# Block keys by DMA, exponential per head and dequantisation shared out between two chunks, in the stage ahead of an attention recurrence

## What is computed

```python
x = x + xattn(layernorm(x), ctx, ctx, mask)      # softmax(q k / 4 + mask) v
x = x + ffn(layernorm(x), gate, up, down)        # int4 weights: q * s, s per 128 inputs
x = x + recurrence(ctx, layernorm(x), lens)      # 256 steps, one after the other
x = x + experts(layernorm(x))                    # 16 experts, top 2
```

## Time and profile before

| what | value |
|---|---|
| median of 3 runs (lowest, highest) | 1523.16 us (1520.36, 1537.06) |
| profiled execution | 1518.94 us |
| its span, first to last instruction | 1516.8 us |
| mean granted clock of TensorE | 0.93 |
| busy over the span | PE 1395.5 us (92%), DVE 943.9 (62%), ACT 544.3 (36%), POOL 275.1 (18%) |
| part A | 0 to 144.43 us |
| part B | 144.43 to 262.83 us |
| part C up to the recurrence's first matmul | 262.83 to 301.66 us |

### The profile page before, as it was taken

One profiled execution on the slowest core, in us unless ns is written; L12 is line 12 of the kernel. 1 busy time (PEld: TensorE's weight loads), 2 busy tenths in 40 slices (PEclk: granted clock), 3 DMA queues, 4 the chain that ended last, 5 costly groups with the idle time before them and its releaser, 6 DMA issues.

```text
span 1516.8 us, 43579 instructions
## 1 busy us (share of the span) xinstructions
PE 1395.5 (92%) x17408; PEld 919.4 (61%) x17408; DVE 943.9 (62%) x4478; ACT 544.3 (36%) x2143; POOL 275.1 (18%) x743
## 2 busy tenths in 40 slices
PE   4743887899999999999999999999999999999988
PEld 2533666466665676666666765556666666666546
DVE  4898455366665666675666657766655566566643
ACT  1343132134333344333334434443433333333321
POOL 3334222211111111111011111231110011111111
PEclk8565797999999999999999999999998999999989
DMA  8623000000000000000000001210000000000000
GB/s 278 240 90 90 0 1 4 1 2 2 3 2 2 2 2 2 3 2 2 2 2 2 2 19 45 58 37 2 2 16 2 2 2 9 9 2 3 9 9 14
DMA packets 19551, 37.06 MB, mean 24 GB/s; under 512 B 8436, under 2 KB 11683, under 8 KB 19348
## 3 DMA queue, kind: packets, MB, share of 16 engines
q1 hardware_dynamic: 19348, 34.28, 6.9%
HBM read 32.18 MB, written 2.10 MB: 23 GB/s over the span
## 4 chain that ended last, share of the span: by engine, by line
PE 83%; DVE 9%; issue 3%; ACT 2%; SPq 1%; POOL 1%; DMA 0%; DVEq 0%; ACTq 0%; POOLq 0%
PE bank L1921 9%; PE bank L1842 9%; PE bank L1635 9%; PE bank L1864 8%; PE bank L1652 6%; PE bank L1896 6%; PE bank L1673 4%; PE bank L1870 4%; PE bank L1618 3%; PE bank L1878 3%; PE bank L1905 3%; PE bank L1884 2%; PE bank L1612 2%; PE bank L1566 2%; PE bank L1518 2%
## 5 line engine op out<-in xcount | busy, mean ns | idle before, releaser
L1842 PE MATMUL bank<-ctx_lgs,identb 128*128 128x512 f16 (+2 forms) x685 | 190.9, 356 | 0.0
L1921 PE MATMUL bank<-ker_mem,uh 128*128 128x128 f32 x1020 | 184.3, 304 | 0.7 <-DVE ker_mem L1121 0.4
L1921 PEld LDWEIGHTS bank<-ker_mem,uh 128*128 128x128 f32 x1020 | 137.0, 194 | 66.1 <-DVE ker_mem L1121 48.9
L1635 PE MATMUL bank<-xT,wbig 128*128 128x256 f16 x1008 | 162.9, 275 | 0.0
L693 POOL TENSOR_TENSOR sscale<-ex,rinv 128x8 f32<-128x8 f32 x256 | 51.0, 199 | 506.8 <-DVE rinv L1106 506.8
L1439 ACT ACTIVATE xs<-gat 64x8 f32<-64x8 f32 x255 | 52.9, 207 | 244.2 <-DVE gat L1117 244.2
L1425 ACT ACTIVATE ker_mem<-bank 128x128 f16<-128x128 f32 x256 | 71.0, 278 | 184.8 <-PE bank L1864 184.8
L1430 ACT ACTIVATE eh<-bank,nmx 128x8 f16<-128x8 f32 x256 | 68.5, 268 | 172.4 <-PE bank L1887 172.4
L689 POOL COPY sscale<-s 64x4 f32<-64x4 f32 x256 | 59.0, 230 | 388.6 <-DVE s L1136 388.6
L1652 PE MATMUL bank<-wbig,interT 128*128 128x512 f16 x378 | 125.6, 399 | 0.0
L1121 DVE TENSOR_TENSOR ker_mem<-inv,ahn 128x128 f32<-128x128 f32 x510 | 124.0, 285 | 0.1
(11 more groups left out here) (238 smaller groups left out, 3290.9 us busy)
## 6 DMA issues: line engine op xcount, KB each, us to landing
wbig<-d_gate_qT SPq DMA_DIRECT2D x4, 896.0 KB, 9.9
wbig<-d_up_qT SPq DMA_DIRECT2D x4, 896.0 KB, 20.7
wbig<-d_down_qT SPq DMA_DIRECT2D x1, 3584.0 KB, 31.5
x_sb<-d_x SPq DMA_DIRECT2D x16, 128.0 KB, 6.0
d_out<-x_sb SPq DMA_DIRECT2D x16, 128.0 KB, 2.3
sscale<-d_gate_sT SPq DMA_DIRECT2D x2, 896.0 KB, 8.3
sscale<-d_up_sT SPq DMA_DIRECT2D x2, 896.0 KB, 4.3
work<-d_g1T SPq DMA_DIRECT2D x8, 224.0 KB, 2.5
```

Of the source, the lines that this page charges most:

```text
L1635: last = mm(tile_bank(n)[:, lo:lo + QC], w[wi][:, kt, it * P:(it + 1) * P], x_part[q % 2][xi][:, kt, :], start=(kt == 0 and wi + xi == 0), ...
L1842: mm(bank[7][:, 0:n], identb[:], hg2[:, 0].rearrange("p h g -> p (h g)")[:, 0:n], start=True, stop=True)
L1921: mm(bank[0][:, 0:P], uh[:, h, :], qv[:, h, :, :], start=False, stop=False, skip_group_check=True)
```

## The change

Six edits, all ahead of the recurrence:

1. The block keys are laid out in DRAM ready-made (`keys`, 4 x 4 blocks of 128 x 512) and loaded by SP (`load_keys`, 256 KB each, 32 loads, one for each score step of both chunks) into four buffers. POOL's `key_block`, krep and headsel are gone. SP issues load n when score n-4 is done.
2. The subtraction on DVE (L768) is gone. The maximum comes out negated, and ACT takes the exponential as eight activations of 64 columns with that maximum as the bias operand.
3. `chunk_steps` staggers chunk 1 as it does chunk 0.
4. `slices_at` is new: slices 0 to 3 stand in tile 0's steps g, 4 to 7 in tile 1's, and 8 to 12, two to a tile, in tiles 4, 5 and 6, in part B.
5. All low halves are on DVE, with one semaphore. Slices from 8 on use two buffers of scales. PE waits for 8 low halves before part B and for all 13 before part C.
6. In each score step that has a layernorm, the moments stand between scaling and maximum; at the ends of part A the layernorms are put in another order. SP loads the down integers behind the keys of chunk 0 and the rest of x.

The core of the diff:

```diff
         def slices_at(k, g, lag):
-            n = KT * (k - 1) + g - lag
-            return [n] if 0 < k < B and n >= 0 else []
+            if k < B:
+                n = 4 * k + g - lag
+                return [n] if 0 <= n < 8 else []
+            n = 8 + 2 * (k - B) + g - lag
+            return [n] if 0 <= g - lag < 2 and n <= LAST else []
...
-                    if c == 0 and b > 0 and j < STEPS // 2:
+                    if b > 0 and j < STEPS // 2:
                         continue
                     next(tiles[b])
                     yield
-                    if c == 0 and b + 1 < B and j >= STEPS // 2:
+                    if b + 1 < B and j >= STEPS // 2:
...
+            def load_keys(n):
+
+                if n >= 4:
+                    sp.wait_ge(s["score_done"], n - 3)
+                sp.dma_start(kbd[:, n % 4, :], a["keys"][n // KT % B, n % KT]).then_inc(kbd_in[n % 4], 16)
...
-            def key_block(k, kt):
-                n = k * KT + kt
-                if n >= 2:
-                    pool.wait_ge(s["score_done"], n - 1)
-                nc.gpsimd.tensor_tensor(
-                    kbd[:, n % 2, :].rearrange("p (h t) -> p h t", h=8),
-                    krep[:, kt, k % B, :].unsqueeze(1).broadcast_to([P, 8, T]),
-                    headsel[:].unsqueeze(2).broadcast_to([P, 8, T]), ALU.mult).then_inc(s["kbd_ready"], 1)
...
-                    sc_max = smax[:, kt * 8:(kt + 1) * 8]
-                    link(nc.vector.tensor_reduce(sc_max, v, AX.X, ALU.max))
-                    nc.vector.tensor_tensor(v, v, sc_max.unsqueeze(2).broadcast_to([P, 8, T]), ALU.subtract).then_inc(s["sub_done"], 1)
+                    if kt == 1 and b < 2:
+                        moments(6 * c + 2 + b, 4 * c + 1 + 2 * b)
+                    dve.wait_ge(s["scaled"], n + 1)
+                    if n >= KT:
+                        dve.wait_ge(s["exp_done"], n - KT + 1)
+                    nc.vector.tensor_reduce(smax[:, kt * 8:(kt + 1) * 8], v, AX.X, ALU.max, negate=True).then_inc(s["max_ready"], 1)
...
-                    act.wait_ge(s["sub_done"], k * KT + kt + 1)
-                    nc.scalar.activation(sc[:, kt, :], sc[:, kt, :], ACT.Exp).then_inc(s["exp_done"], 1)
+                    act.wait_ge(s["max_ready"], k * KT + kt + 1)
+                    for h in range(8):
+                        cols = slice(h * T, (h + 1) * T)
+                        last = nc.scalar.activation(sc[:, kt, cols], sc[:, kt, cols], ACT.Exp, bias=smax[:, kt * 8 + h:kt * 8 + h + 1])
+                    last.then_inc(s["exp_done"], 1)
```

More of the change, by code:

```diff
@@ L99, in build @@
         minus_half = sb("minus_half", [P, 1])
-        krep = sb("krep", [P, KT, B, T])
-        headsel = sb("headsel", [P, 8])
-        kbd = sb("kbd", [P, 2, 512])
+        kbd = sb("kbd", [P, 4, 512])
         vbd = sb("vbd", [P, B, 8, 34])
@@ L281, in build @@
         x_in = [sem(f"s_x{i}") for i in range(4)]
+        kbd_in = [sem(f"s_kbd{i}") for i in range(4)]
         block = ctx.enter_context(nc.Block())
@@ L449, in _ @@
             load_x(2, x_in[1])
-            sp.dma_start(headsel[:], a["c_headsel"]).then_inc(s["attn_in"], 16)
-            sp.dma_start(krep[:], a["krep"]).then_inc(s["attn_in"], 16)
+            load_keys(0)
             for h in range(2):
@@ L466, in _ @@
                 if n < 4:
-                    sp.dma_start(scales[n], a["gate_sT"][n:n + 1, :].partition_broadcast(P)).then_inc(w_sc[n], 16)
-            sp.dma_start(in_tiles(wbig[:, 2 * nw:], IT0).bitcast(I32), a["down_qT"].rearrange("(k p) o -> p k o", p=P)).then_inc(w_in[8], 16)
+                    load_scales(n)
+            for n in (4, 5, 6, 7, 8, 9):
+                load_keys(n)
+            load_scales(4)
+            load_keys(10)
+            load_scales(5)
+            load_keys(11)
+            load_keys(12)
+            load_scales(6)
+            load_keys(13)
+            load_scales(7)
+            load_keys(14)
+            load_keys(15)
             for slot in (4, 6, 5, 7):
                 load_x(slot, x_in[3])
-            for n in range(4, 8 + len(DPART)):
-                sp.wait_ge(s["low_odd" if n % 2 else "low_ready"], n // 2 - 1)
-                if n < 8:
-                    sp.dma_start(scales[n % 4], a["up_sT"][n % 4:n % 4 + 1, :].partition_broadcast(P)).then_inc(w_sc[n % 4], 16)
-                else:
-                    i0, i1 = DPART[n - 8]
-                    sp.dma_start(scales[n % 4][:, 0:(i1 - i0) * H],
-                                 a["down_sT"][i0:i1, :].rearrange("g h -> (g h)").unsqueeze(0).partition_broadcast(P)).then_inc(w_sc[n % 4], 16)
+            sp.dma_start(in_tiles(wbig[:, 2 * nw:], IT0).bitcast(I32), a["down_qT"].rearrange("(k p) o -> p k o", p=P)).then_inc(w_in[8], 16)
+            load_scales(8)
+            load_scales(9)
+            for n in range(16, 24):
+                load_keys(n)
+            load_scales(10)
+            load_keys(24)
+            load_scales(11)
+            for n in range(25, 28):
+                load_keys(n)
+            load_scales(12)
+            for n in range(28, 32):
+                load_keys(n)
             sp.dma_start(lys[:], a["LysT"].rearrange("(k p) o -> p k o", p=P)).then_inc(s["rec_in"], 16)
@@ L563, in attention @@
                         rstd_of(4)
-                    for n in slices_at(k, g, 2):
-                        if n % 2 == 0:
-                            low_part(n)
                     yield
@@ L741, in low_part @@
                 dve.wait_ge(s["high_ready"], n + 1)
-                nc.vector.tensor_tensor(low, product, high, ALU.subtract).then_inc(s["low_odd"], 1)
+                nc.vector.tensor_tensor(low, product, high, ALU.subtract).then_inc(s["low_ready"], 1)
             def input_low(q, p, bk, kts=slice(0, KT), final=True):
@@ L805, in _ @@
             dve.wait_ge(x_in[0], 32)
-            layernorm(0, 0)
+            moments(0, 0)
             dve.wait_ge(x_in[1], 32)
-            layernorm(1, 2)
+            moments(1, 2)
+            normalise(0, 0)
+            normalise(1, 2)
             dve.wait_ge(x_in[2], 64)
@@ L1485, in attention @@
                     for i in range(2):
-                        if c == 1 and b == 0:
-                            pe.wait_ge(s["xl_ready"], i + 1)
+                        if c == 1:
+                            pe.wait_ge(s["scaled"], KT * k - 1 + i)
+                            pe.wait_ge(s["pt_copied"], 4 * B)
                         transposes(n0 + i, attention_bank(k, 0, n0 + i))
@@ L1987 @@
     kT = ctx.reshape(B, T, 8, HD).transpose(2, 3, 0, 1)
-    krep = np.repeat(kT[:, None], 4, 1).reshape(KT, P, B, T).transpose(1, 0, 2, 3)
+    krep = np.repeat(kT[:, None], 4, 1).reshape(KT, P, B, T)
+    keys = np.zeros((B, KT, P, 8, T), np.float32)
+    for h in range(8):
+        rows = slice(h * HD, (h + 1) * HD)
+        keys[:, :, rows, h] = krep[:, rows].transpose(2, 0, 1, 3)
     arrays = {
-        "x": i["x"], "ctx_1024": ctx, "mask_SxS2_ff0": i["mask_SxS2_ff0"], "krep": krep,
+        "x": i["x"], "ctx_1024": ctx, "mask_SxS2_ff0": i["mask_SxS2_ff0"], "keys": keys.reshape(B, KT, P, 8 * T),
         "lens": i["_lenS2"].reshape(B, 1),
```

75 lines of the change are left out of this document (36 added, 39 removed).

## The result

| | before | after |
|---|---|---|
| median (lowest, highest) | 1528.12 us (1520.36, 1537.06), 4 runs | 1508.45 us (1504.97, 1511.63), 4 runs |
| profiled execution, span | 1518.94, 1516.8 us | 1507.64, 1505.8 us |
| granted clock over the span | 0.93 | 0.94 |
| part A | 144.4 us | 137.5 us |
| part B | 118.4 us | 109.2 us |

The ratio of the medians is 0.9876, with a 95% interval of 0.9828 to 0.9923. The change makes the kernel 1.2% faster, 12 to 26 us by the interval. The recurrence starts 15.0 us earlier; 28.9 had been forecast.

What follows compares the result with a forecast made beforehand. DVE was taken to bound part A and PE part B, partly through its lower clock level. Gains of 12.4 and 16.5 us, 28.9 together, cut the span from 1516.8 to 1487.9, giving 1492 us, range 1470 to 1515.

Steps and rivals of the forecast that it cites:

- The keys of tile 1: Part A: tile 1's first key queues behind gate and up integers, landing at about 47; a new wait of some 15 us.
- POOL's low halves: Part A: each low half on POOL costs DVE about 3.4 us, while DVE does one itself in 2.30.
- PE is now denser than before, so I take part of it: Part A: some upper-level clock on PE ends the part at 132 instead of the walk's 136.7.
- Only the scales of slice 6 ... come 2 to 3 us late: Part A: slice 6's scales, queued behind key 12, arrive 2 to 3 us late, already counted in the 132.
- The walk: Part A: following DVE's and PE's queues, PE at the lower level throughout, puts the end at 136.7.
- DVE's work left, 71.6: Part A: DVE's remaining work sums to 71.6 us; DVE alone would end at 120.5.
- The wait at the turns: Part B: products wait 3.6 us at three tile turns; with 5 us elsewhere, 16 us of PE idle time.
- For the surcharge I take half of what it was, 13: Part B: PE's extra time at the lower clock level falls from 25.2 us to 13.
- Eight exponentials in 1.7 us: ACT's eight 64-column activations start 0.21 us apart, 1.7 us in all, making the next link 0.4 us later.
- differs by more than 3 us: Sign of being wrong: part C or the recurrence, where no change was counted, differs by more than 3 us.
- the clock eats it: Rival, chance 0.18: part A stays at the lower level (7.7 gained), part B takes 118.9; 7.2 gained in all, 1514.
- The slower case: Rival, chance 0.05: waits at turns and DVE's new slices keep PE at 0.50; part B takes 150, total 1540.

Runs made afterwards that it cites:

- keys_early: The changed kernel with the keys of tile 1 loaded ahead of the up integers, behind the gate's: 1497.14 us, ratio to before 0.9797.
- low_on_dve: The kernel before with one edit, POOL's seven low halves given to DVE: 1521.11 us, ratio to before 0.9933.
- after_again: The changed kernel run once more without any edit: 1510.09 us, ratio to before 0.9876.
- no_stagger: The changed kernel with chunk 1's tiles one after the other again: 1519.17 us, ratio to before 0.9976.
- keys_scales_one_exp: The changed kernel with tile 1's keys and slices 6 and 7's scales loaded earlier, subtraction on DVE and one exponential: 1493.55 us, again 1493.46; ratios 0.9762, 0.9767.

## Why the prediction was right and wrong

It forecast 1492 us, 1470 to 1515, and faster by over 1% with 0.80. The time is inside the range, the sign is right, and the 1.2% are at the border of what was called measurable. The gain was half the forecast's: the start of the recurrence moved by 15.0 and not 28.9 us. The profiled span came out 17.9 above the forecast's 1487.9: part A 5.5, part B 7.3, part C 1.2, the recurrence 4.0.

- **The keys of tile 1: right.** Forecast 47, measured 46.5; nothing overtook. (54.8 less 8.9 is 45.9 and not 45.5; it changes nothing.) That the wait hides nothing is shown too, by keys_early.
- **POOL's low halves: right.** 3.4 us lost for each, and low_on_dve shows 3.4. In the changed kernel no operation of 512 columns on DVE ahead of the recurrence is longer than 0.78 us, where one was 4.13.
- **"PE is now denser than before, so I take part of it": a term of part A that was too large.** It took 4.7 us off for the upper level. The clock did rise, from 0.57 to 0.65, and after_again shows what the level is worth: 2.3 us, between tile 2's and tile 3's first products. The stretch of tile 3's products behind it, which the forecast counted too, ran near the lower level in both profiles (0.51 and 0.52 from 118 to 137). (That part A was at 0.57 "throughout" before is a mean; from 80 to 100 it was at 0.67.)
- **"Only the scales of slice 6 ... come 2 to 3 us late": a term of part A that was too small.** The wait was 6.3 us, and 3.9 and 4.3 in the two other profiles of the same code. The walk had the load behind key 12 rightly. But key 12 waits for a score that ends only at 74.05, and from its issue at 74.46 the load took 7.5 us.
- **The walk: close, partly by luck.** With PE at the lower level throughout, it had the eighth low half end at 102, tile 2's last product at 111, tile 3's at 127 and part A at 136.7; measured are 104.0, 111.4, 127.8 and 137.5. But the measured times have the upper level's 2.3 us in them, which the walk left out, and DVE had less to do than it assumed; both hide the longer wait for scales.
- **DVE's work left, 71.6: too much,** at 63.5. From the eighth low half on, DVE is not the bound but a link. PE waited 27.4 us in late part A for ACT's copy, and its longest wait, 7.4, follows DVE's for the scales:

```profile
PE bank L1539 <- ACT interT L1225: 27.4, 8, 7.4
```

- **The wait at the turns: right in sum.** Forecast three of 3.6 and 16 us of idle time; measured 3.52, 2.26 and 5.03, and 16.7. DVE's work in part B, put at 70, was 61.0; it did not bound.
- **"For the surcharge I take half of what it was, 13": the term of part B that was too small.** It was 92.5 - 72.9 = 19.6, 6.6 of the 7.3 us missed. Of the 25.2 before, the changed kernel gave back 5.6 and not 12.2. The reason given, that the longest wait falls from 5.4 to 3.6, did not hold: one was 5.0, and the stretch around it ran at 0.66. The mean of the waits was right and told nothing of the longest. It is not the chance of one profile: part B took 109.1 to 109.7 us in all five that have it unedited, at 0.81 or 0.82.
- **Eight exponentials in 1.7 us: wrong.** They take 2.02. The Trainium skill (ScalarE: Activation LUTs, What ACT_TABLE_LOAD costs) had the better number. An estimate from its figures is 280 + 53 = 333 ns for one of 64 columns, and 240 ns apart. The trace agrees, with 335 and 241. The two of 8 columns were no guide to the distance of longer ones. In part B eight exponentials instead of one cost 1.4 to 5.1 us (109.1 to 109.7 against 104.6, 106.3 and 107.7), in PE's busy time at a lower clock and not in its idle time.
- **Part C: 1.2 us longer, not foreseen.** The same 1.2 stand in low_on_dve, which has neither stagger, keys nor exponentials of the change. Of it 0.8 is PE's wait for POOL's ctx_lgs at the start of the part, 5.8 us instead of 5.0. In after_again the wait was 5.0, so it differs from execution to execution; the cause stays open.
- **The recurrence: 4.0 us longer in the profile.** Nothing in it is edited; in after_again it took 1223.2. Its spread is larger than this, and so the sign "differs by more than 3 us" could not tell right from wrong.

Of the other signs, the first gate/up matmul at 137.5 is just outside its 125 to 137, the eight activations are outside, and of the three waits only one lay at 3 to 4 us. DVE waited for no scales in part B, as forecast.

The rival "the clock eats it" (1514) was nearer to the measured 1508 than the forecast (1492), and that is partly luck. Its part A came true in size (6.9 gained, 7.7 said), though not in its reason, since the clock rose. Its part B did not (118.9 said, 109.2 measured): the surcharge fell, though less than forecast. That the sum is near all the same is due to part C and the recurrence, which took 5.2 us more than before. The slower case is not what happened, but no_stagger comes near its mechanism: with the other five edits alone the start is 6.5 us earlier, and the ratio does not tell the kernel from the one before (0.9948 to 1.0005). Edits 3, 4 and 5, the exponentials of edit 2 and the order of the loads were run by themselves; `load_keys` against `key_block` and the new places of the layernorms were not.

## What to carry to other kernels

Before you replace a small computation by a load, look at what the queue holds at that point: here four loads of 256 KB behind the weights cost 16 us, and moving them and two loads of scales ahead brought 19.5 us of the start, where all six edits had brought 15.0. A second engine that helps beside the first can cost it more than it takes off: each low half on POOL lost DVE 3.4 us, where DVE does one in 2.3, and giving DVE its whole work back shortened part A by 9.8 us. Before you read a difference of 2 us between two profiles, compare a stretch of unedited code in both, with its granted clock and with the waits for loads in front of it: here two executions agreed to 0.05 us because two differences of 2.3 us cancelled.

## What the runs showed of the hardware

- The same code got a different granted clock in different executions. Between tile 2's and tile 3's first products it was 0.85 to 0.87 in three profiles and 0.57 or 0.58 in three others, and the stretch took 18.7 to 18.9 us or 21.0. PE was busy 12.0 to 12.2 us of it or 17.6: of 5.6 us, 2.3 reached the end of the stretch, because PE otherwise waits between its steps.
- A load issued at the same time (74.46, 74.55) on the same queue was used at 82.05 or 79.72.
- A low half on POOL (4.0 to 4.6 us for 128 x 1792) slowed DVE's work beside it by 3.4 us on average, over six of them, two of these narrower.
- The same recurrence took from 1215 to 1240 us. The four executions of keys_scales_one_exp went with the clock: 1485.24 us is the fastest and 1506.92, at a granted clock of 0.920, the slowest. A gain of 4 us at the start needs the profile to be seen.
- A queued load is late by all that stands ahead of it: the same four keys let the score start at 46.5 behind eight slices of weights and at 37.6 behind four; behind two, at 29.8, the score did not wait for them.
